# One of seven pair tiles through layer 1 as a single f32 matmul, in a recommender kernel on Trainium2

## The reference, cut to what matters

```python
e = jnp.stack([tbl_0[ids[:, 0]], ..., tbl_38[ids[:, 38]]], axis=1)      # (512, 39, 16) f32
x1 = jnp.einsum('bid,bjd,ijh->bhd', e, e,  W0.reshape(39, 39, 128))     # layer 1
x2 = jnp.einsum('bid,bjd,ijh->bhd', e, x1, W1.reshape(39, 128, 128))    # layer 2
z = jnp.sum(jnp.concatenate([x1, x2], axis=1), axis=-1)                 # (512, 256)
h = jnp.concatenate([z, dense_ctx], axis=1)                             # (512, 272)
h = jnp.maximum(h @ W_top1 + b_top1, 0.0)
h = jnp.maximum(h @ W_top2 + b_top2, 0.0)
y = h @ W_top3                                                          # (512, 1)
```

## Time and profile before

| | |
|---|---|
| three runs | 290.53, 290.00, 289.96 us, median 290.0 |
| span of the profiled execution, first to last instruction | 288.8 us |
| difference of the median from that span | 1.2 us |
| instructions | 4761 |
| mean granted TensorE clock | 0.959 of full speed |
| PE / PEld busy | 232.4 us (80%) / 190.2 us (66%) |
| DVE / ACT / POOL busy | 182.3 (63%) / 171.9 (60%) / 141.6 us (49%) |

### The profile page before, as it was taken

The page is one execution under the profiler, slowest core; times in us unless marked ns, Lnnn a source line. Parts: engine busy times, 40 slices in busy tenths (PEclk is TensorE's granted clock), DMA queues, the critical chain, the costliest instruction groups (busy, mean ns, idle before and its releaser), DMA issues.

```text
span 288.8 us, 4761 instructions
## 1 busy us (share of the span) xinstructions
PE 232.4 (80%) x1548; PEld 190.2 (66%) x1548; DVE 182.3 (63%) x325; ACT 171.9 (60%) x314; POOL 141.6 (49%) x135
## 2 busy tenths in 40 slices
PE   0001259389999599999995999999959999999897
PEld 0001258146778479678784796787847967878696
DVE  6566560697987555668865566688664666875301
ACT  1133142898995872868948728689477286885301
POOL 4777787787877777777787777400000000000000
PEclk9999999659999989999999899999997999999999
DMA  4433732972221200320220002202100022022000
GB/s 77 113 120 123 179 101 48 291 192 51 55 52 17 44 7 6 56 52 6 53 51 6 6 6 52 50 0 45 43 2 1 3 45 48 0 45 47 1 2 0
DMA packets 28978, 15.14 MB, mean 52 GB/s; under 512 B 20559, under 2 KB 26793, under 8 KB 28961
## 3 DMA queue, kind: packets, MB, share of 16 engines
q1 hardware_dynamic: 24768, 13.84, 18.4%
q0 software_dynamic: 4192, 1.08, 4.8%
HBM read 9.66 MB, written 0.00 MB: 33 GB/s over the span
## 4 chain that ended last, share of the span: by engine, by line
PE 74%; ACT 9%; SPq 7%; DMA 5%; issue 2%; DVE 2%; ACTq 0%
PE turn_bank L356 12%; PE pair_bank L294 9%; PE x_bank L316 9%; PE x_bank L319 8%; PE x_bank L318 7%; SPq L227 6%; DMA tab<-small 5%; ACT x L692 5%; PE turn_bank L368 4%; PE g_bank L343 4%; PE g_bank L347 3%; PE g_bank L344 3%; PE x_turn_bank L329 3%; PE turn_bank L396 2%; PE turn_bank L286 2%
## 5 line engine op out<-in xcount | busy, mean ns | idle before, releaser
L265 POOL DMA_INDIRECT emb<-tbl,ids_sb x131 | 141.4, 1079 | 43.0 <-issue 39.0
L710 ACT ACTIVATE prod<-pair_bank 128x512 f32<-128x512 f32 (+1 forms) x112 | 65.6, 599 | 13.7 <-PE pair_bank L294 12.3
L568 DVE TENSOR_TENSOR prod_lo<-prod,prod_hi 128x512 fp32r<-128x512 f32 x96 | 62.0, 687 | 1.5
L316 PE MATMUL x_bank<-prod_hi,pair_w_hi 128*128 128x512 f32 (+1 forms) x112 | 61.9, 553 | 0.7 <-DVE prod_lo L568 0.4
L294 PE MATMUL pair_bank<-x,sel 117*128 117x512 bf16 (+1 forms) x112 | 46.9, 423 | 15.9 <-ACT x L692 11.2
L717 ACT ACTIVATE prod_hi<-prod 128x512 fp32r<-128x512 f32 x64 | 40.2, 633 | 0.5
L319 PE MATMUL x_bank<-prod_hi,pair_w_lo 128*128 128x512 f32 x96 | 38.4, 400 | 0.0
L318 PE MATMUL x_bank<-prod_lo,pair_w_hi 128*128 128x512 f32 x96 | 38.3, 399 | 0.0
L356 PE MATMUL turn_bank<-g_sb,w_sb 128*128 128x128 f32 x312 | 35.7, 276 | 0.6 <-ACT g_sb L751 0.6
L356 PEld LDWEIGHTS turn_bank<-g_sb,w_sb 128*128 128x128 f32 x312 | 35.1, 192 | 1.1 <-ACT g_sb L751 0.9
L439 PE MATMUL pair_bank<-tab_parts,onehot 125*128 125x48 bf16 x160 | 6.5, 211 | 35.9 <-ACT tab_parts L797 35.9
(11 more groups left out here) (91 smaller groups left out, 320.8 us busy)
## 6 DMA issues: line engine op xcount, KB each, us to landing
xblk<-xs SPq DMA_DIRECT2D x64, 80.0 KB
emb<-tbl,ids_sb POOLq DMA_INDIRECT x131, 3.9
tab<-small SPq DMA_DIRECT2D x2, 625.0 KB
wt<-w_top SPq DMA_DIRECT2D x2, 512.0 KB
small_ids_i<-small_ids SPq DMA_DIRECT2D x2, 500.0 KB
small_ids_i<-small_ids SPq DMA_DIRECT2D x1, 562.5 KB
tab<-small SPq DMA_DIRECT2D x1, 562.5 KB
wa<-pair_w_a SPq DMA_DIRECT2D x1, 448.0 KB
```

What stands on the lines that cost most here:

```text
L265: pool.indirect_dma_start(out=emb[:, at:at + D], out_offset=None, in_=tables[f], in_offset=bass.IndirectOffsetOnAxis(ap=ids_sb[:, c * M + ...
L316: mm = pe.matmul(x1_bank[:, :], pair_w_hi[p, t, :], prod_hi[p, j % 2, t, :], start=(n == 0), stop=(n == FULL))
L568: dve.tensor_tensor(prod_lo[:, j % 2, t, :] if t < FULL else prod_hi[rows, j % 2, t, :], prod[rows, t, :], prod_hi[rows, j % 2, t, :], ALU ...
L710: act.activation(prod[0:ROWS[t], t, :], pair_bank[(j * NT + t) % 2][0:ROWS[t], :], ACT.Square).then_inc(sq_done, 1)
```

## The change

Tile 4 (`WHOLE`), the fifth of a block, is no longer split. ACT writes its square in f32 into a buffer of its own, `prod_whole` (one for even and one for odd blocks). ACT's rounding of it and DVE's `take_lo` for it fall away. `layer1` for it is one f32 matmul with f32 weights `pair_w_whole`, which ACT copies from `pair_w` once at the start, in place of the three fp32r matmuls. The counts of `hi_act` and `lo_done` per block fall by one, and `layer1` for tile 4 waits for `sq_done` instead of `lo_done`. The square of tile 4 waits for `x1_mm` of two blocks back instead of `lo_done`. The full diff:

```diff
--- before.py
+++ after.py
@@ -35,8 +35,10 @@
 LEFT = PAIRS - 128 * FULL
 ROWS = [128] * FULL + [96]
 DVE_ROUNDS = (1, 3, 5)
-ACT_TO = [n - sum(m < n for m in DVE_ROUNDS) for n in range(NT + 1)]
-DVE_TO = [n - ACT_TO[n] for n in range(NT + 1)]
+WHOLE = 4
+DVE_TO = [sum(m < n for m in DVE_ROUNDS) for n in range(NT + 1)]
+ACT_TO = [n - DVE_TO[n] - (n > WHOLE) for n in range(NT + 1)]
+LO_TO = [n - (n > WHOLE) for n in range(NT + 1)]
 DVE_X1_AT = 2
 LAG = 2
 MO = M + 1
@@ -74,6 +76,7 @@
         pair_w_hi = sb("pair_w_hi", [128, NT, H], F32R)
         pair_w_lo = sb("pair_w_lo", [128, FULL, H], F32R)
         touch = sb("touch", [128, NT, M])
+        pair_w_whole = sb("pair_w_whole", [128, H])
         sel = sb("sel", [P3, NT, 128], BF16)
         wt1 = sb("wt1", [128, 2, F1])
         wtd = sb("wtd", [DENSE, F1])
@@ -117,6 +120,7 @@
 
 
         prod = sb("prod", [128, NT, COLS])
+        prod_whole = sb("prod_whole", [128, 2, COLS])
         prod_hi = sb("prod_hi", [128, 2, NT, COLS], F32R)
         prod_lo = sb("prod_lo", [128, 2, FULL, COLS], F32R)
         g_sb = sb("g_sb", [128, MO, CH])
@@ -309,7 +313,12 @@
 
                 k = NB * c + j
                 t = n
-                pe.wait_ge(lo_done, NT * k + n + 1)
+                if t == WHOLE:
+
+                    pe.wait_ge(sq_done, NT * k + n + 1)
+                    pe.matmul(x1_bank[:, :], pair_w_whole[:, :], prod_whole[:, j % 2, :], start=False, stop=False)
+                    return
+                pe.wait_ge(lo_done, (NT - 1) * k + LO_TO[n + 1])
                 if n == 0:
                     wait(pe, x1_kept, k)
                 p = slice(0, ROWS[t])
@@ -447,7 +456,7 @@
             for t in range(NT):
                 select_pair(0, 0, t)
             turn_x(0, 0)
-            pe.wait_ge(pair_w_split, 2)
+            pe.wait_ge(pair_w_split, 3)
             later_blocks(0, False)
             pe.wait_ge(w1_in, 16)
             pe.wait_ge(mlp_in, 16 * 7)
@@ -561,7 +570,7 @@
                 if t in DVE_ROUNDS:
                     dve.wait_ge(hi_dve, len(DVE_ROUNDS) * k + DVE_TO[t + 1])
                 else:
-                    dve.wait_ge(hi_act, (NT - len(DVE_ROUNDS)) * k + ACT_TO[t + 1])
+                    dve.wait_ge(hi_act, (NT - 1 - len(DVE_ROUNDS)) * k + ACT_TO[t + 1])
                 wait(dve, x1_mm, k - 1)
 
                 rows = slice(0, 128) if t < FULL else slice(32, 64)
@@ -573,7 +582,7 @@
                 for n in range(n0, n1):
                     if n - 1 in DVE_ROUNDS:
                         round_hi(c, j, n - 1)
-                    if n >= LAG:
+                    if n >= LAG and n - LAG != WHOLE:
                         take_lo(c, j, n - LAG)
 
             def take_xs_lo(c, j):
@@ -706,8 +715,11 @@
             def square(c, j, t):
                 n = NT * (NB * c + j) + t
                 act.wait_ge(pair_sel, n + 1)
-                wait(act, lo_done, n + 1 - NT)
-                act.activation(prod[0:ROWS[t], t, :], pair_bank[(j * NT + t) % 2][0:ROWS[t], :],
+                if t == WHOLE:
+                    wait(act, x1_mm, NB * c + j - 1)
+                else:
+                    wait(act, lo_done, (NT - 1) * (NB * c + j - 1) + LO_TO[t + 1])
+                act.activation(prod_whole[:, j % 2, :] if t == WHOLE else prod[0:ROWS[t], t, :], pair_bank[(j * NT + t) % 2][0:ROWS[t], :],
                                ACT.Square).then_inc(sq_done, 1)
 
             def round_hi(c, j, t):
@@ -721,7 +733,7 @@
                 for n in range(n0, n1):
                     if n < NT:
                         square(c, j, n)
-                    if n >= 1 and n - 1 not in DVE_ROUNDS:
+                    if n >= 1 and n - 1 not in DVE_ROUNDS and n - 1 != WHOLE:
                         round_hi(c, j, n - 1)
 
             def keep_x1h(c, j):
@@ -823,6 +835,7 @@
             keep_turned(0)
             act.wait_ge(pair_w_done, 1)
             act.activation(pair_w_hi[:, :, :], pair_w[:, :, :], ACT.Copy, scale=0.5).then_inc(pair_w_split, 1)
+            act.activation(pair_w_whole[:, :], pair_w[:, WHOLE, :], ACT.Copy, scale=0.5).then_inc(pair_w_split, 1)
             tiles(0, 0, 0, NT + 1)
             round_xs(0, 0)
             later_blocks(0, False, "late")
@@ -843,7 +856,7 @@
                 keep_g(c - 1, 3, 2)
                 square(c, 0, 4)
                 for t in range(4):
-                    if t not in DVE_ROUNDS:
+                    if t not in DVE_ROUNDS and t != WHOLE:
                         round_hi(c, 0, t)
                 tiles(c, 0, 5, NT + 1)
                 keep_z2(c - 1)
```

## The result

The changed kernel takes 293.88 us (median of four runs, 293.48 to 294.55) against 289.98 us (289.21 to 290.53): a ratio of 1.013, with an interval of 1.010 to 1.0155. It is slower, by 3.9 us in this comparison. The forecast was 293.3 us. The profiled execution has a span of 291.7 us, 2.9 us more than the one before, and took 293.48 us.

What follows compares the result with a forecast made beforehand. PE's matmul stream was taken to bound the kernel, with ACT and DVE mostly beside the path. Terms +3.2 (f32 matmul), +0.2 (copy) and -0.1 (relief) made +3.3 us on 290.0: 293.3 us, 8-in-10 range 291.6 to 294.3.

Steps and rivals of the forecast that it cites:

- PE bounds the blocks: In the blocks PE, busy 232.4 of 288.8 us, sets the pace; DVE and ACT are mostly beside the path.
- An f32 matmul streams four times: Tile 4's layer-1 f32 matmul of 512 columns costs four streamings, two recorded halves of 0.449 us each.
- The reading from the group with 39 weight columns: Early f32 matmuls with shorter weight loads keep 0.114 us per half, so moving columns, not loads, set the pace.
- the cheap rival: Tile 4's f32 matmul costs only 0.47 or 0.58 us, giving 286.5 or 288.3 us; chance 7%, faster.
- the price of the f32 matmul: In layer 1, 0.90 us per block replaces 0.70 us of three fp32r matmuls: 16 x 0.20 = +3.2 us.
- The lower bound named: Four bare streamings of 512 columns at 2.4 GHz, 0.85 us per f32 matmul; +2.4 us over sixteen blocks.
- The copy at the start: ACT's 128x128 copy of f32 weights before the first block lies on the path: +0.2 us (0.1 to 0.3).
- The relief: ACT's rounding and DVE's subtraction removed per block: 0.1 us gained, bounds nothing to 2.0 us; larger relief had 8%.
- The sum: Whole kernel: 3.2 + 0.2 - 0.1 = +3.3 us, added to the 290.0 us median, giving 293.3 us.
- The clock: Half-clock stretches after PE's three gaps: one fewer gives 291.7 us, one more 294.9; chance 8% in all, slower.
- a sign of being wrong: In the changed kernel's profile, a number of half-clock stretches other than three beside the first would refute the prediction.
- the difference of a median and another execution's span: Whole kernel: the median was taken to lie 1.2 us above the profiled span, with nothing outside the span changing.

Runs made afterwards that it cites:

- the second job: Four variants against the kernel before (289.75 us): changed kernel with f32 matmul twice 307.22, on two tiles 296.16, cut in two 293.97; rounded matmuls cut 291.14.
- The three comparisons: The unaltered changed kernel against the kernel before, in three jobs: 293.88 against 289.98 us, 435.85 against 433.11, 293.67 against 290.56.
- the repeat: The changed kernel again, unaltered, against the kernel before in the third job: 293.67 us against 290.56, ratio 1.011.
- the padded one: The kernel before with the 16-row dense part of the top layer's first matmul padded with zero rows to 128: 285.42 us against 290.56, ratio 0.984.

## Why the prediction was right, point by point

**PE bounds the blocks: right, and shown in the traces.** Keeping the rounding and subtraction beside the f32 matmul moved no distance between two layers 2 by more than 0.02 us, and taking them out beside three rounded matmuls by 0.03 us at most. 8 us of DVE and 7 us of ACT work vanished without a trace in these distances.

**An f32 matmul streams four times: right.** The reading from the group with 39 weight columns held: at 512 columns it is 0.86 us, against 0.47 and 0.58 of the cheap rival, which is refuted.

**The term that was mis-sized is the price of the f32 matmul, 0.90 us, and with it +3.2 us.** It is 0.86, so 16 x 0.16 = +2.6 us. The prediction scaled the whole pace of the 128-column halves by columns, also the part above bare streaming, 0.1123 - 0.1067 = 0.0056 us. That part does not grow with the columns: the second job shows 0.43 us per half of 512, where the scaled price is 0.449. The lower bound named, 0.85 us, was nearly exact.

**The copy at the start: on the path, but 0.07 us and not 0.2.** Its 0.19 us in the chain was read rightly; the squares behind it gave 0.11 us of it back.

**The relief: 0.1 us was taken, some 0.04 us measured.**

**The sum.** With these terms the change is 2.6 + 0.07 - 0.04 = +2.6 us where +3.3 was predicted. The three comparisons gave +3.9, +2.7 and +3.1 us. The second and third agree with it inside their intervals (1.8 to 3.9 and 2.1 to 4.4 us). The first does not quite, as its interval begins at 2.9 us. All four of its runs lie at 293.5 us and above, where the repeat had four of six. That the forecast of 293.3 came so near to 293.88 is partly luck, an overpriced f32 matmul beside an unpriced clock.

**The clock: a rival that came true in part.** The prediction allowed one stretch of 1.65 us more or less, from a trace with three equal ones. It also named as a sign of being wrong that the stretches at half clock are not three beside the first; the clock row after has one more, in slices 5 and 6. The runs show more kinds: a clock that rises ahead of the f32 stream before the first block or inside it (0.69 us), and 3.4 or 10.2 us around a gap. The long one cost 0.59 us in the first gap after and 59.63 - 58.59 = 1.04 us in the second of the repeat. And runs of the kernel before differ by up to 2.6 us in one job, where the prediction leaned on three that agreed to 0.6. Neither kind belongs to the change alone. The f32 stream of 28 halves took 4.20 us in the run with the rounded matmuls cut in halves and 3.53 in the padded one, which have no f32 matmul in layer 1, and 3.19 in the runs with the f32 matmul twice and with two whole tiles. The first two also have half clock from 96 to 104 us. Whether the changed kernel meets bad places more often than the one before stays open, with one trace of each kernel per job.

**An execution stands 1.8 us and not 1.2 us above its span.** After, 293.48 - 291.7 = 1.8 us, for the same execution. The prediction added the difference of a median and another execution's span. As the forecast was made by adding to the median, nothing came of it.

## What to carry to other kernels

When TensorE sets the pace, count streamings: here one f32 matmul was four, three rounded ones were three, and what the trade frees on VectorE and ScalarE is worth only what TensorE is seen to wait for them. To price a matmul of a size that the trace lacks, take bare streaming by columns as the lower bound and the small one's pace scaled by columns as the upper: here the excess of an f32 half did not grow with its columns, and that of a rounded matmul did, so neither rule is safe alone. Then look at every group of the same kind, for one with another pace (here L368) shows a cost that can be removed. And measure the spread of the kernel before first: with 2.6 us between its own runs, a change of 2.6 us needs the distances inside the trace to be understood.

## What the runs showed of the hardware that was not expected

- At full clock a matmul that streams its 512 columns once, bf16 or fp32r, takes 0.233 us in the stream, where 512 columns at 2.4 GHz are 0.213. A half of an f32 matmul takes 0.43, where two streamings are 0.427. The excess of the first kind goes with columns (two of 256 take 0.235), and at half clock it is gone: 0.43 us from one rounded matmul of 512 to the next (95.64, 96.07 and 96.49 us in the trace after), where 1.2 GHz gives 0.427. Why is not shown.
- f32 weight loads behind a change between 16 and 128 rows came 0.19 us later than others, 24 times in the loop, in all 4.35 us of 290, removed by rows of zeros. The Trainium skill ("TensorE: Matmul & The Clock Gate", section "The mechanism") lists that a weight load overlaps matmuls in flight only where the row groups differ. The trace does not agree with that line: loads of the same 128 rows, 0.19 us long, follow each other every 0.11 us beside the matmuls, and those behind a change of the row count come later. The same section also has a load pulled ahead when it goes to the background weight buffer, which would allow the first; of the second it says nothing.
- In one job PE's matmuls of the look-up came with 48 to 54 waits of 2.2 to 2.3 us on average for nothing that the profile shows, 111 to 123 us in all, in each of the four kernels profiled there; the kernel before was as long (433 us). The cause is not known.
- The granted clock that a profile shows early in a kernel can be at odds with the pace: 1.00 and 0.50 from 38 to 42 us in the two traces, and 0.039 us for each look-up matmul in both, where those at full clock behind them took 0.025.
